# A fused decoder layer on one core: the self-attention's step rewritten with its mask added by VectorE, and the openings of three phases

## The chip, the cores and the metric

The kernel runs on one core of a Trainium2 chip. The metric is the time of one execution on the device in microseconds (us). TensorE (PE) multiplies matrices, VectorE (DVE), ScalarE (ACT) and GpSimd (POOL) work on tiles of 128 partitions, and SyncE (SP) issues most transfers between the chip's memory (HBM) and the core. Each engine runs its own queue of instructions in order; engines wait for each other through semaphores.

## The reference

One decoder layer, all in float32, for x of 4 x 512 tokens x 512 features:

```
x = x + self_attention(layernorm(x))
x = x + cross_attention(layernorm(x), ctx)
x = x + feed_forward(layernorm(x))

self_attention(h):                      # 16 heads of 128, one key and one value head
    q = rmsnorm(rope(h @ wq_comp @ wq_up)) * q_norm_w      # 16 heads
    k = rmsnorm(rope(h @ wk)) * k_norm_w;  v = h @ wv
    scores = q k^T / sqrt(128);  scores = where(0 <= i - j < 128, scores, -1e30)
    probs = softmax([scores, sink_logit])[..., :t]
    return (group_of_4_heads(probs @ v) @ out_w1[group]) @ out_w2
cross_attention(h, ctx):                # 16 query heads of 32, 4 key heads, 1024 keys
    softmax(q k^T / sqrt(32) + slope_h * (j - i), masked) @ v @ Wo
feed_forward(h):                        # 512 -> 2048 -> 512, 8-bit activations, ternary weights
    z = silu(bitlinear(h, w_gate)) * bitlinear(h, w_up)
    return bitlinear(fwht(z), w_down)   # fwht: Walsh-Hadamard transform over 2048
```

## The kernel before

The program has three phases, one after the other, each with a block of code per engine. Matrices that need float32 accuracy are kept as two rounded halves (`_hi`, made by ScalarE with a Copy, and `_lo`, the difference, made by VectorE), and a product is three matmuls, hi x hi, lo x hi and hi x lo (the helper `three`, L640 to L642).

**Self-attention** (`phase_self_attention`, L114) works on 16 tiles of 128 tokens. The window of 128 keys means that a tile sees its own 128 keys and the 128 before (256 keys in 12 of the tiles, 128 in the first tile of each batch of 512 tokens). A tile has 4 steps, one for each group of 4 heads, so there are 64 steps c = 0 to 63. Every engine's block runs the same loop `for c in CS` with c from -9 to 66 (L249), and in one pass of it does parts of several steps: the scores of step c, the query transposes of c+1, the probability transposes of c-1, the head outputs `ps_a` and the output product `ps_out` of steps before, the query projection `ps_up` of c+3, and on some steps the projections of a later tile. The order within a pass is the order of the code, and it sets the order on each queue.

The mask of a step is put down by TensorE: before the scores, two matmuls of the identity with the mask's window (`ident_r`, `window_r`, L690) write -1e30 or 0 into `ps_s`, and the score matmuls add to that. VectorE then takes the maximum of the four heads in one instruction (L538), forms the negated maximum times the norm factor (four small instructions, L542), ScalarE makes the exponentials (L442, one for each head), VectorE the reciprocal of the sum, GpSimd multiplies (L634) and TensorE transposes the result (L710).

In the opening (c = -8 to -1) TensorE also multiplies out_w1 by out_w2, so that the output product of a head is one matrix of 128 x 512: two heads in each pass (`merged_heads`, L257), 4 matmuls a head, in float32 (L674). The weights of a group of 4 heads are 2 MB, loaded in 2 transfers (`load_merge`).

**Cross-attention** (`phase_cross_attention`, L784) runs over 64 heads (4 batches x 16), each in 4 units of 128 queries; the scores of a unit are 2 matmuls of 512 keys. Scores are computed twice, once for the maximum (L1435, read by VectorE L1286) and once with the maximum folded in (L1418, read by ScalarE). Queries and keys are made by projections, split, stored to HBM in part and read back by SP into the stacked operands `Q` and `K` (`spread_queries`, `spread_keys`). In the opening the first head's queries are written into `Q` by ScalarE and VectorE; the others come by DMA. The rows of the next batch are loaded by `load_x1` (L924) and measured by VectorE (`statistics`, L1157).

**Feed-forward** (`phase_feed_forward`, L1513) runs over 16 tiles of 128 tokens, 4 quarters each. The last stages of the Walsh-Hadamard transform, sums and differences between quarters (`between_quarters`, L1783, into `fC` and `fA`) and between halves (`between_halves`, L1798, into `fB`), are made by GpSimd for every tile, and TensorE transposes `fB` (L1830).

The order in all three phases is written out by hand in these loops; there is no scheduler.

## Time and profile before

| | us |
|---|---|
| three runs | 1744.24, 1746.03, 1747.74 |
| median | 1746.03 |
| profiled execution | 1742.52 |
| its span | 1740.7 |
| PE busy | 1632.4 (94%) |
| DVE busy | 1202.6 (69%) |
| ACT busy | 1238.6 (71%) |
| POOL busy | 1184.2 (68%) |

The span is the time from the first to the last instruction that the profiler recorded; the profiled execution's own time is 1.8 us more. The self-attention takes the span's first 665 us or so, the cross-attention goes on to about 1400, and the feed-forward fills the rest. Busy shares are averages over these stages. The rows below come from four views: the busy time of each engine in stretches, instructions grouped by line, the waits of an engine, and the timeline of single stretches. In a row of the timeline the first number is the start, the second the duration of the whole entry (which may stand for several instructions, x2), and in square brackets stands how long the engine was idle before and what released it.

### The profile page before, as it was taken

What the parts mean: (1) busy time and instruction counts of PE and PEld (TensorE: products, weight loads), DVE (VectorE), ACT (ScalarE), POOL (GpSimd) and SP (SyncE); (2) the same over time, 40 slices, a digit from 0 to 9 for tenths busy, and PEclk for the clock granted to TensorE, in tenths of its full rate; (3) what the DMA queues carried; (4) which work ended last, traced back from release to release, by engine and by line L of the source; (5) the groups of instructions that cost most, each with busy time, mean ns of one, the idle gap of its engine ahead of it and who ended that gap; (6) DMA issues with size and microseconds to landing.
All of it is one profiled execution on the core that took longest, in us unless ns stands there. A gap on an engine that the chain in (4) does not pass through costs nothing. (4 is left out here: it accounts for less than half of the span.)

```text
span 1740.7 us, 24610 instructions
## 1 busy us (share of the span) xinstructions
PE 1632.4 (94%) x7920; PEld 1147.5 (66%) x7920; DVE 1202.6 (69%) x2284; ACT 1238.6 (71%) x2022; POOL 1184.2 (68%) x1085
## 2 busy tenths in 40 slices
PE   6999989999999997799999999999999977999996
PEld 3488878888888875566656665666556534666664
DVE  2378778677766665668787778777787735777764
ACT  2366577888666653589788778888897845787875
POOL 0377877777887762457666666666776739888892
PEclk9999999999999998899999999999999999999999
DMA  6214234333300102411141113101200320001000
GB/s 231 97 61 87 98 104 123 103 94 115 110 13 7 37 7 51 132 42 34 28 122 46 34 34 115 28 28 40 60 24 25 140 109 1 26 26 36 25 20 25
DMA packets 57215, 110.32 MB, mean 63 GB/s; under 512 B 9180, under 2 KB 13660, under 8 KB 56704
## 3 DMA queue, kind: packets, MB, share of 16 engines
q1 hardware_dynamic: 55536, 107.84, 20.1%
q8 instruction: 65, 1.06, 0.3%
q10 hardware_dynamic: 1552, 0.91, 0.2%
q14 instruction: 62, 0.51, 0.1%
HBM read 71.10 MB, written 18.88 MB: 52 GB/s over the span
## 5 line engine op out<-in xcount | busy, mean ns | idle before, releaser
L1351 POOL TENSOR_TENSOR x_p_lo<-x_p,x_p_hi 128x1024 fp32r<-128x1024 f32 x192 | 455.3, 2385 | 232.8 <-ACT x_p_hi L1148 232.4
L1286 DVE TENSOR_REDUCE x_maxes<-x_ps_a 128x1 f32<-128x1024 f32 x252 | 306.9, 1218 | 150.8 <-PE x_ps_a L1435 145.8
L1121 ACT ACTIVATE x_p<-x_ps_b,x_any_valid 128x1024 f32<-128x1024 f32 x256 | 285.1, 1114 | 128.8 <-PE x_ps_b L1418 113.7
L1418 PE MATMUL x_ps_b<-x_Q,x_K 100*128 100x512 f32 x512 | 228.1, 527 | 7.0 <-ACT x_p L1121 4.4
L1148 ACT ACTIVATE x_p_hi<-x_p 128x1024 fp32r<-128x1024 f32 x192 | 203.2, 1058 | 4.8
L1435 PE MATMUL x_ps_a<-x_K,x_Q 99*128 99x512 f32 x504 | 165.9, 410 | 11.2 <-DVE x_maxes L1286 9.0
L1464 PE MATMUL x_ps_o<-x_p_hi,x_V 128*96 128x512 f32 x384 | 156.7, 408 | 1.2 <-POOL x_p_lo L1351 1.2
L1418 PEld LDWEIGHTS x_ps_b<-x_Q,x_K 100*128 100x128 f32 x512 | 89.9, 191 | 99.8 <-issue 74.4
L1465 PE MATMUL x_ps_o<-x_p_lo,x_V 128*96 128x512 f32 x384 | 151.1, 393 | 0.0
L442 ACT ACTIVATE a_work<-a_ps_s,a_neg_max,a_q_r 128x256 f32<-128x256 f32 (+1 forms) x256 | 134.1, 540 | 4.6 <-DVE a_neg_max L542 4.6
L634 POOL TENSOR_TENSOR a_work<-a_work,a_inv_den 128x1024 f32<-128x1024 f32 (+1 forms) x64 | 110.0, 1719 | 18.6 <-DVE a_inv_den L582 18.6
L1435 PEld LDWEIGHTS x_ps_a<-x_K,x_Q 99*128 99x128 f32 x504 | 90.5, 191 | 48.0 <-DVE x_maxes L1286 26.9
L1469 PE MATMUL x_ps_o<-x_p,x_V 128*96 128x512 f32 x256 | 120.4, 591 | 0.0
L623 POOL TENSOR_TENSOR a_q_r<-a_q_ss,a_half_neg 128x4 f32<-128x4 f32 x64 | 65.2, 1018 | 75.5 <-DVE a_q_ss L560 73.8
L640 PE MATMUL a_ps_out<-a_w_hi,a_aT_hi 128*128 128x512 f32 x256 | 108.5, 424 | 1.4 <-DVE a_aT_lo L503 1.4
L642 PE MATMUL a_ps_out<-a_w_hi,a_aT_lo 128*128 128x512 f32 x256 | 102.9, 402 | 0.0
L641 PE MATMUL a_ps_out<-a_w_lo,a_aT_hi 128*128 128x512 f32 x256 | 102.5, 400 | 0.0
L427 ACT ACTIVATE a_qT_hi<-a_ps_front 128x512 fp32r<-128x512 f32 x64 | 38.3, 598 | 64.3 <-PE a_ps_front L701 64.3
L1296 DVE CAST x_Q<-x_ps_x 4x128 fp32r<-4x128 f32 x256 | 74.1, 289 | 9.3 <-PE x_ps_x L1447 1.3
L1464 PEld LDWEIGHTS x_ps_o<-x_p_hi,x_V 128*96 128x96 f32 x384 | 62.2, 162 | 26.5 <-POOL x_p_lo L1351 2.0
L609 POOL TENSOR_TENSOR a_work<-a_q 128x512 f32<-128x512 f32 x64 | 66.5, 1040 | 18.9 <-ACT a_q L465 18.9
L503 DVE TENSOR_TENSOR a_aT_lo<-a_ps_a,a_aT_hi 128x512 fp32r<-128x512 f32 x64 | 44.2, 691 | 49.5 <-ACT a_aT_hi L386 49.1
(254 smaller groups left out, 4353.3 us busy)
## 6 DMA issues: line engine op xcount, KB each, us to landing
shared<-in_L_attn_out_w SPq DMA_DIRECT2D x8, 1024.0 KB, 7.3
shared<-in_L_ffn_w_gate SPq DMA_DIRECT2D x16, 512.0 KB, 4.3
shared<-in_L_ffn_w_up SPq DMA_DIRECT2D x16, 512.0 KB, 4.1
shared<-in_L_ffn_w_down SPq DMA_DIRECT2D x16, 512.0 KB, 4.0
shared<-in_ctx SPq DMA_DIRECT2D x8, 1024.0 KB, 7.5
x_scratch<-rows SPq DMA_DIRECT2D x31, 256.0 KB, 2.0
x_Q<-x_q_hi SPq DMA_DIRECT2D x112, 64.0 KB, 2.0
ffn_quant<-shared SPq DMA_DIRECT2D x24, 256.0 KB, 4.6
```

Of the source, the lines that this page charges most:

```text
L442: act.activation(p[:, c % 2, j, 0:w], ps_s[:, j, 0:w], ACT.Exp, scale=q_r[:, c % 4, j:j + 1], bias=neg_max[:, c % 2, j:j + 1], accum_out=r ...
L634: pool.tensor_tensor(out=p[:, c % 2, :, 0:w], in0=p[:, c % 2, :, 0:w], in1=inv_den[:, c % 2, :].unsqueeze(2).to_broadcast([P, G1, w]), op= ...
L640: pe.matmul(out_ap, hi, rhs_hi, start=start, stop=False)
L1121: act.activation(p[:, r, :, :], ps_b[:, :, :], ACT.Exp, scale=any_valid[:, b % 2:b % 2 + 1]).then_inc(exp_ready, 1)
L1148: act.activation(p_hi[:, r], p[:, r], ACT.Copy).then_inc(hi_ready, 1)
L1286: dve.tensor_reduce(out=maxes[:, c % 2, 32 * r + 3:32 * r + 4], in_=scores_bank(n)[:, :, :], axis=mybir.AxisListType.XY, op=ALU.max).then_ ...
L1351: pool.tensor_tensor(out=p_lo[:, r], in0=p[:, r], in1=p_hi[:, r].bitcast(F32), op=ALU.subtract).then_inc(lo_ready, 1)
L1418: last = pe.matmul(ps_b[:, j, :], K[0:ROWS + 4, g, kb * P:(kb + 1) * P], Q[0:ROWS + 4, hh, :], start=True, stop=True)
L1435: last = pe.matmul(scores_bank(n)[:, j, :], Q[0:ROWS + 3, h2, r * P:(r + 1) * P], K[0:ROWS + 3, g2, j * 512:(j + 1) * 512], start=True, st ...
L1464: pe.matmul(bank[0:ROWS, :], vs, p_hi[:, rw, j], start=(rw == 0 and j == 0), stop=False)
L1465: last = pe.matmul(bank[0:ROWS, :], vs, p_lo[:, rw, j], start=False, stop=False)
L1469: last = pe.matmul(bank[0:ROWS, :], V32[:, bw % 2, j, gw, :], p[:, 3, j], start=False, stop=(j == 1))
```

## The change

It has five parts.

1. **Mask.** The two mask matmuls of each step and their operands go. The score matmuls start `ps_s` themselves. VectorE negates the window once, and in each step runs one `tensor_tensor_reduce` for each head, which adds the window to the scores in PSUM, writes them back there and takes their maximum.
2. **Order of a step.** On TensorE the head outputs `ps_a` of step c-2 come behind the scores of step c (they stood at the end of the pass before, as step c-1), and the output product of c-2 goes to the pass's end. The matching splits move on ScalarE and VectorE, the query's norm factor is negated one pass later, and GpSimd's power (`a_q_r`) comes behind its multiply.
3. **Opening of the self-attention.** The merge of the first group's 4 heads is all done at c = -8, chunk by chunk, each of 4 chunks (256 KB of out_w1 and 256 KB of out_w2) with a semaphore of its own, and without waiting for the constants; then two heads in each of c = -7 to -2, none at c = -1. Loads are issued in another order, and four splits are made later.
4. **Opening of the cross-attention.** Two heads' queries are written on the chip instead of one; the second query projection is cut into four pieces that stand between the scores of c = -2; SP loads the next batch's rows ahead of the last keys and Wo; the next batch's statistics start one head later.
5. **Feed-forward.** For tiles 0 and 15 the second `between_quarters` and both `between_halves` run on VectorE.

```diff
 # part 1, VectorE
-                    dve.tensor_reduce(out=s_max[:, c % 2, :], in_=ps_s[:, :, 0:w], axis=AXX, op=ALU.max).then_inc(s_max_ready, 1)
+                    for j in range(G1):
+                        dve.tensor_tensor_reduce(out=ps_s[:, j, 0:w], in0=ps_s[:, j, 0:w], in1=window[:, 2 * P - w:], scale=1.0,
+                                                 scalar=-3.0e38, op0=ALU.add, op1=ALU.max,
+                                                 accum_out=s_max[:, c % 2, j:j + 1]).then_inc(s_max_ready, 1)
 # parts 1 and 2, TensorE
-                    for j in range(0, G1, 2):
-                        pe.matmul(ps_s[:, j:j + 2, 0:w], ident_r[:, :], window_r[:, 2 * P - w:].unsqueeze(1).to_broadcast([P, 2, w]),
-                                  start=True, stop=False)
                     for j in range(G1):
                         last = three(ps_s[:, j, 0:w], qT_hi[:, c % 2, j, :], qT_lo[:, c % 2, j, :], kT_hi[:, keys], kT_lo[:, keys],
-                                     False, j % 2 == 1)
+                                     True, True)
...
 # part 2, VectorE
+                if 0 <= c - 2 < STEPS:
+                    k = c - 2
+                    dve.wait_ge(aT_hi_ready, k + 1)
+                    dve.tensor_tensor(out=aT_lo[:, k % 2, :], in0=ps_a[:, :], in1=aT_hi[:, k % 2, :].bitcast(F32), op=ALU.subtract)\
+                        .then_inc(aT_lo_ready, 1)
                 if 0 <= c + 1 < STEPS:
                     k = c + 1
+                    dve.wait_ge(q_r_ready, k + 1)
+                    dve.tensor_scalar(neg_r[:, k % 4, :], q_r[:, k % 4, :], -1.0, None, ALU.mult).then_inc(neg_r_ready, 1)
 # part 3, SyncE and TensorE
-            load_merge(0)
+            for k in range(DC):
+                sp.dma_start(w1_raw[:, 0, k, :], w1t[0, k * P:(k + 1) * P, :]).then_inc(w12_chunk_in[k], 16)
+                sp.dma_start(w2_raw[:, 0, k, :], w2[k * P:(k + 1) * P, :]).then_inc(w12_chunk_in[k], 16)
...
-            pe.wait_ge(const_in, 96)
-            pe.wait_ge(round_ready, 3)
             for c in CS:
-                for m in merged_heads(c):
+                if c == -8:
+                    for k in range(DC):
+                        pe.wait_ge(w12_chunk_in[k], 32)
+                        for m in merged_heads(c):
+                            last = pe.matmul(merge_bank(m), w1_raw[:, 0, k, m * P:(m + 1) * P], w2_raw[:, 0, k, :],
+                                             start=(k == 0), stop=(k == DC - 1))
...
+                    pe.wait_ge(const_in, 96)
+                    pe.wait_ge(round_ready, 1)
 # part 4, ScalarE, TensorE
+            act.wait_ge(first_q_made, 1)
+            for j in range(2):
+                act.activation(Q[0:DH, j, :], ps_j[j * DH:(j + 1) * DH, :], ACT.Copy, scale=QSCALE).then_inc(first_heads_hi_ready, 1)
...
                     if n == 4:
+                        pe.wait_ge(first_heads_dup_ready, 2)
+                        pe.wait_ge(first_heads_lo_ready, 2)
+                    if n == 8:
                         pe.wait_ge(q_spread[0], queries_spread(0, 0))
...
+                if c == -2:
+                    last = pe.matmul(ps_x[:, :], wq_sb[:, r, P:2 * P], hT[:, r, :], start=(r == 0), stop=(r == DC - 1))
 # part 5, VectorE (and the same condition negated on GpSimd)
+        VECTOR_TILES = (0, TILES - 1)
+                if i == 0 and quarter(c, 4) and n - 1 in VECTOR_TILES:
+                    between_quarters(dve, n - 1, 2)
+                if i == 1 and quarter(c, 5) and n - 1 in VECTOR_TILES:
+                    between_halves(dve, n - 1, 0)
+                    between_halves(dve, n - 1, 1)
```

TensorE's queue around the scores of a step in the self-attention's middle, before. The names are the product and its operands, so `a_ps_s` are scores, `a_ps_front` the query transposes, `a_ps_pT` those of the probabilities:

```order
L690 MATMUL a_ps_s<-a_window_r,a_ident_r 128x512 x2
L640 MATMUL a_ps_s<-a_kT_hi,a_qT_hi 128x256
L641 MATMUL a_ps_s<-a_kT_lo,a_qT_hi 128x256
L642 MATMUL a_ps_s<-a_kT_hi,a_qT_lo 128x256
...
L701 MATMUL a_ps_front<-ident,a_q 128x128 x4
L710 MATMUL a_ps_pT<-ident,a_work 128x128 x8
```

The same place after:

```order
L646 MATMUL a_ps_s<-a_kT_hi,a_qT_hi 128x256
L647 MATMUL a_ps_s<-a_kT_lo,a_qT_hi 128x256
L648 MATMUL a_ps_s<-a_kT_hi,a_qT_lo 128x256
...
L646 MATMUL a_ps_a<-a_pT_hi,a_v_hi 128x512
L647 MATMUL a_ps_a<-a_pT_lo,a_v_hi 128x512
L648 MATMUL a_ps_a<-a_pT_hi,a_v_lo 128x512
...
L722 MATMUL a_ps_front<-ident,a_q 128x128 x4
L731 MATMUL a_ps_pT<-ident,a_work 128x128 x8
```

The two mask matmuls are gone, and the six matmuls of `ps_a` (two blocks of keys, three each; one block is shown, and one head of the scores) now stand between the scores and the query transposes.

VectorE's queue in one step, before:

```order
L538 TENSOR_REDUCE a_s_max<-a_ps_s 128x4
L542 TENSOR_SCALAR a_neg_max<-a_s_max,a_neg_r,a_neg_sinks 128x1 x4
L547 TENSOR_TENSOR a_qT_lo<-a_ps_front,a_qT_hi 128x512
L553 TENSOR_TENSOR a_pT_lo<-a_ps_pT,a_pT_hi 128x1024
L558 TENSOR_REDUCE a_q_ss<-a_work 128x4
L560 TENSOR_SCALAR a_q_ss<-a_q_ss 128x4
L579 TENSOR_SCALAR a_neg_r<-a_q_r 128x4
L582 RECIPROCAL a_inv_den<-a_den 128x4
```

And after; the first two rows, an operation over one head's scores and the reading of its accumulator, stand four times in the queue:

```order
L537 ISA a_ps_s,a_s_max<-a_ps_s,a_window 128x256
L537 ISA a_s_max 128x1
...
L543 TENSOR_SCALAR a_neg_max<-a_s_max,a_neg_r,a_neg_sinks 128x1 x4
L548 TENSOR_TENSOR a_aT_lo<-a_ps_a,a_aT_hi 128x512
L553 TENSOR_SCALAR a_neg_r<-a_q_r 128x4
L555 TENSOR_TENSOR a_qT_lo<-a_ps_front,a_qT_hi 128x512
L560 TENSOR_REDUCE a_q_ss<-a_work 128x4
L562 TENSOR_SCALAR a_q_ss<-a_q_ss 128x4
L582 RECIPROCAL a_inv_den<-a_den 128x4
L587 TENSOR_TENSOR a_pT_lo<-a_ps_pT,a_pT_hi 128x1024
```

One instruction has become eight, the split of `ps_a` came down from ahead of them, and the split of the probabilities went behind the reciprocal.

## Rows read from the trace of the kernel before

**Rows 1.** Busy time by stretch; columns: stretch, length, engines (instructions), PE clock, DMA share, GB/s.

```profile
0.00:81.00 81.00, 64.66 (x176) 32.24 (x176) 23.02 (x51) 22.55 (x47) 13.85 (x30) 1.00 0.44 153
81.00:240.00 159.00, 149.16 (x863) 129.55 (x864) 126.68 (x284) 100.09 (x277) 124.94 (x192) 0.98 0.30 88
240.00:440.00 200.00, 186.70 (x1066) 162.01 (x1066) 148.18 (x351) 160.58 (x373) 152.98 (x233) 0.98 0.38 112
440.00:645.00 205.00, 198.50 (x1148) 171.36 (x1148) 137.61 (x321) 125.49 (x345) 158.15 (x235) 1.00 0.11 36
665.00:720.00 55.00, 39.96 (x149) 27.36 (x150) 35.40 (x55) 20.18 (x24) 16.08 (x9) 0.81 0.37 101
720.00:1380.00 660.00, 654.86 (x2495) 410.03 (x2494) 503.76 (x739) 549.59 (x598) 448.41 (x198) 1.00 0.19 56
```

**Rows 2.** Instructions by line, 80 to 660 us; busy total, mean ns, idle before.

```profile
L538 DVE TENSOR_REDUCE a_s_max<-a_ps_s 128x4 f32<-128x1024 f32 (+1 forms) x64 | 69.4, 1085 | 8.3 <-PE a_ps_s L642 8.2
...
L690 PE MATMUL a_ps_s<-a_window_r,a_ident_r 128*128 128x512 f32 (+1 forms) x128 | 36.9, 370 | 1.8 <-ACT a_work L442 0.9 <-DVE a_qT_lo L547 0.9
```

**Rows 3.** Waits of TensorE, 100 to 640 us; total us, times, longest.

```profile
PE a_ps_front L701 <- DVE a_kT_lo L523: 12.1, 13, 2.0
...
PE a_ps_front L701 <- DVE a_hT_lo L508: 3.8, 13, 0.6
...
PE a_ps_front L701 <- DVE a_v_lo L513: 2.9, 1, 2.9
```

**Rows 4.** Timeline of one step of the self-attention and the start of the next.

```profile
442.62 0.62 PE L690 MATMUL a_ps_s<-a_window_r,a_ident_r 128*128 128x512 f32 x2
443.08 0.28 PE L640 MATMUL a_ps_s<-a_kT_hi,a_qT_hi 128*128 128x256 f32 x1
...
444.71 1.23 DVE L538 TENSOR_REDUCE a_s_max<-a_ps_s 128x4 f32<-128x1024 f32 x1 [0.16 <-PE a_ps_s L642]
445.97 0.82 DVE L542 TENSOR_SCALAR a_neg_max<-a_s_max,a_neg_r,a_neg_sinks 128x1 f32<-128x1 f32 x4
...
447.63 0.56 ACT L442 ACTIVATE a_work<-a_ps_s,a_neg_max,a_q_r 128x256 f32<-128x256 f32 x1
...
453.62 0.28 DVE L520 TENSOR_TENSOR a_qcT_lo<-a_ps_front,a_qcT_hi 128x128 fp32r<-128x128 f32 x1
453.82 0.28 DVE L523 TENSOR_TENSOR a_kT_lo<-a_ps_front,a_kT_hi 128x128 fp32r<-128x128 f32 x1
```

**Rows 5.** Busy time by stretch, the first 10 us.

```profile
0.00:5.00 5.00, 0.00 (x0) 0.00 (x0) 0.09 (x2) 0.71 (x1) 0.20 (x4) 1.00 0.52 160
5.00:10.00 5.00, 0.00 (x0) 0.00 (x0) 0.00 (x0) 0.57 (x1) 0.00 (x0) 1.00 1.04 369
```

**Rows 6.** Timeline of the self-attention's opening.

```profile
15.46 8.65 PE L674 MATMUL a_ps_s<-shared 128*128 128x512 f32 x16 [15.46 <-ACT a_window_r L374]
...
26.00 1.90 DVE L478 TENSOR_TENSOR a_w_lo<-a_work,a_w_hi 128x512 fp32r<-128x512 f32 x3 [0.53 <-ACT a_w_hi L378]
...
80.91 0.50 PE L690 MATMUL a_ps_s<-a_window_r,a_ident_r 128*128 128x256 f32 x2 [0.87 <-DVE a_qT_lo L547]
...
82.78 1.00 DVE L579 TENSOR_SCALAR a_neg_r<-a_q_r 128x4 f32<-128x4 f32 x1 [1.13 <-POOL a_q_r L623]
```

**Rows 7.** Timeline of the cross-attention's opening.

```profile
679.56 3.60 PE L1398 MATMUL x_ps_x<-x_hT,shared 128*128 128x512 f32 x8
...
689.56 1.22 PE L1435 MATMUL x_ps_a<-x_K,x_Q 99*128 99x512 f32 x2 [1.99 <-DMA x_Q<-x_p_lo]
...
711.88 0.69 DVE L1157 BATCH_NORM_STATS2 x_stats<-shared 128x6 f32<-128x512 f32 x1 [9.37 <-DMA shared<-x_scratch]
...
713.96 1.22 PE L1435 MATMUL x_ps_a<-x_K,x_Q 99*128 99x512 f32 x2 [5.26 <-DVE x_maxes L1286]
```

**Rows 8.** Timeline of the feed-forward's first tile.

```profile
1440.55 1.27 POOL L1788 TENSOR_TENSOR f_fC<-f_f 128x512 f32<-128x512 f32 x1
...
1445.70 4.66 POOL L1801 TENSOR_TENSOR f_fB<-f_fA 128x1024 f32<-128x1024 f32 x2
1448.09 0.66 PE L1830 MATMUL f_ps_t<-ident,f_fB 128*128 128x128 f32 x4 [4.53 <-POOL f_fB L1801]
```

More of the change, by code:

```diff
@@ L214, in phase_self_attention @@
         w12_in = [sem(f"w12_in{j}") for j in range(2)]
+        w12_chunk_in = [sem(f"w12_chunk_in{k}") for k in range(DC)]
         x_in = [sem(f"x_in{j}") for j in range(XR1)]
@@ L762, in _ @@
                     last.then_inc(qckT_made, 1)
[L763 to L772 removed]
+                if 0 <= c - 2 < STEPS:
+                    k = c - 2
+                    t, g = divmod(k, 4)
+                    pe.wait_ge(aT_lo_ready, k + 1)
+                    if g == 0 and t:
+                        pe.wait_ge(x1_ready, t)
+                    for j in range(G1):
+                        hh, cols = G1 * g + j, slice(j * P, (j + 1) * P)
+                        last = three(ps_out[:, :], aT_hi[:, k % 2, cols], aT_lo[:, k % 2, cols], w12_hi[:, hh, :], w12_lo[:, hh, :],
+                                     hh == 0, hh == H1 - 1)
+                    if g == 3:
+                        last.then_inc(out_made, 1)
 HX, HPG, DH = 16, 4, 32
@@ L967, in spread_queries @@
                 hi, lo = q_stage(g, b)
-                for j in range(1 if b == g == 0 else 0, HPG):
+                for j in range(2 if b == g == 0 else 0, HPG):
                     rows = slice(j * DH, (j + 1) * DH)
@@ L1353, in _ @@
                     normalise((c - 8) // HPG)
-                if 0 <= c < HEADS and b + 1 < B and (hh, r) == (1, 0):
+                if 0 <= c < HEADS and b + 1 < B and (hh, r) == (1 if b else 2, 0):
                     deviations(b + 1)
```

250 lines of the change are left out of this document (120 added, 130 removed).

## The prediction

> **What bounds the kernel now.** I read the busy time by stretch first. TensorE is busy for 149 of 159 us, 187 of 200 and 198.5 of 205 in the self-attention, and for 655 of 660 in the cross-attention's long middle [rows 1]. The change does not touch that middle, so what it can give lies in the self-attention, in the two openings (65 of 81 us, 40 of 55) and at the feed-forward's ends. The grouping by line then gives the price of the mask on TensorE and of the maximum on VectorE [rows 2], TensorE's waits say what it stands for inside the self-attention [rows 3], and the timelines show one step and the three places in the openings [rows 4, 6, 7, 8]. A step lasts (646 - 81) / 64 = 8.83 us. VectorE, which gets the new work, is the next engine: 80% busy from 81 to 240, 74% to 440, 67% to 645 [rows 1], which is 7.1, 6.55 and 5.9 us of a step.
>
> **Self-attention, what goes from TensorE.** With two blocks of keys, the mask's two matmuls start at 442.62 and the scores at 443.08: 0.46 us of the queue [rows 4]. 48 steps of this form give 22.1 us; the 16 steps with one block write half as much, about 0.3 each, 4.8 us. That is 27 us; the row of the line says 36.9 over 128 matmuls [rows 2], but those durations overlap the next matmul, so I go by the starts. TensorE is the busiest engine and in order, so this is taken from the path unless something else becomes late.
>
> The new place of ps_a fills a hole. TensorE waits for the splits of a tile's projections before its query transposes: 12.1 + 3.8 + 2.9 = 18.8 us in 27 waits [rows 3], none over 2.0 us but one. The six matmuls of ps_a (c-2), 6 x 0.23 = 1.4 us at the spacing of the mask's 512-wide ones (0.46 for two [rows 4]), stand in front of these transposes now and need only what is older. 18.8 us is the most they can hide, and 1.4 x 27 covers most of it. Together -45.8 is the lower end.
>
> **What VectorE takes on.** One maximum of 1.23 us [rows 4] becomes four passes over 128 x 256 with a second operand, and four accumulator reads. No such instruction is in the trace. The nearest rows: two 128 x 128 subtractions from PSUM start 0.20 apart, at 453.62 and 453.82 [rows 4]; three 128 x 512 ones take 1.90, 0.63 each [rows 6]. A straight line between them puts 256 columns at 0.35, and a 128 x 1 instruction of the kind behind neg_max costs 0.82 / 4 = 0.2 [rows 4], as an upper value for the accumulator read; 0.07 is what a read could cost if it ran beside the next pass. So 0.42 to 0.55 a head, 1.7 to 2.2 a step. I take 2.0, against 1.23: +0.8 us on VectorE a step. The other bound is a pass at half the rate because it reads PSUM, reads SBUF and writes PSUM: 0.63 + 0.2 = 0.83 a head, 3.3 a step. There is no gain below 1.23, as the same columns go through with more instructions.
>
> The rows show that a second short instruction starts before the first one's 0.28 us are over: starts 0.20 apart [rows 4]. The Trainium skill (VectorE: DVE Perf Modes, "Rules for kernel authors") advises to minimize the number of chained VectorE operations, because each pays for its pipeline's flush; that speaks against making eight of one. By it a head would cost its full duration, about 0.42, and a full 0.2 for the read, near 0.6, 2.5 us a step, between my value and the upper bound. The Trainium skill (Vector Engine (DVE) Microarchitecture Reference, "7. Points that are easy to get wrong") says that this family of operations halves its throughput with two SBUF sources that are not bf16; here one source is in PSUM, so it should be spared, and if the rule holds for this pair too the result is the second rival below. No row here shows either.
>
> With +0.8, VectorE needs 7.9 us of a step early and 6.7 late, where TensorE alone would take about 8.83 - 45.8 / 64 = 8.1. At 94% and above VectorE's order delays what TensorE waits for. I set this friction at 0.35 us for the first 18 steps (6.3) and 0.17 for the other 46 (7.8), 14 us, an estimate from the present gaps: today at 80% the loss of TensorE is 10 of 159 us [rows 1], 0.55 a step. The cycle that could bind instead is scores of step c, maximum, neg_max, exponentials, scores of c+1: 1.45 + 2.0 + 0.82 + four exponentials of 0.56 [rows 4] + some 0.35 of hand-over = 6.9 us, below 8.4; up to 3.4 us of masked maximum it does not decide. Moving the split of the probabilities behind the reciprocal and the negated factor one pass later costs no instruction: TensorE needs pT_lo only for ps_a, which is now a whole pass later, and the wait for GpSimd's power, 1.13 us in the opening [rows 6], goes. GpSimd loses nothing.
>
> Self-attention: -27 - 19 + 14 = **-32** (from -45 to +3, the upper end with the pass at 0.83).
>
> **Opening of the self-attention.** TensorE starts at 15.46, released by the constants' last copy [rows 6]. After, it needs x's first transfer, whose 0.26 MB go ahead, and the first chunk, 0.52 MB; the constants' 0.58 MB travel beside them, so 0.78 to 1.38 MB must land. 160 GB/s in the first 5 us are 0.80 MB, and then 369 GB/s [rows 5]: from 5.0 to 6.6 us. I take 6.2, -9.3 us at the start. A chunk comes every 0.52 MB / 369 GB/s = 1.42 us and TensorE needs 8.65 / 16 x 4 = 2.2 us for its 4 matmuls [rows 6], so nothing waits behind. Then the last pass has no merges, which stood beside the chain from projection to the first scores (they wait 0.87 us for qT_lo at 80.91 already [rows 6]); about 2 us come back there. **-7** (from -9.3 to -3).
>
> **Opening of the cross-attention.** From 665 to 720 TensorE is idle for 15.0 of 55 us, and the clock is at 0.81, between its levels of 1.2 and 2.4 GHz [rows 1]. Three things go: the second projection, 3.6 us in the row at 679.56, leaves the way to the first scores and fills the gaps of the pass c = -2 (worth 1.5, as the keys' splits come after it anyway); the wait of 1.99 us for the first DMA of `x_Q` at 689.56; and the wait of 5.26 us at 713.96, which follows VectorE's 9.37 us for the next batch's rows [rows 7]. SP now issues these loads before the last keys, and the statistics come one head later, some 5 us. I count 5.3 + 2.0 + 1.5 = 8.8, and with fewer gaps 1.2 of the clock's loss: **-10**. At -4 the wait at 713.96 only moves to the keys (0,2), which now stand behind four loads of 256 KB; at -16 most of the idle time goes.
>
> **Feed-forward.** For tile 0 GpSimd needs from 1440.55 to 1445.70 for the quarters and 4.66 for both halves; TensorE starts 4.53 us late at 1448.09 [rows 8]. VectorE makes the four quarter operations at 0.63 each [rows 6], 2.5 us, with a product of 0.7 among them, then a half (twice the columns) at 1.2: the first half is there at about 1445.1, -3. Tile 15 does the same by the same code near the very end, where I count -1. VectorE's other work there is that product and small rows. **-4** (-8 to -1).
>
> **Sum.** 1742.5 - 32 - 7 - 10 - 4 = 1689.5 by the profiled execution. The median of the runs is 3.5 us above that execution, so I predict 1689.5 + 3.5 = 1693 us.
>
> **Rivals.**
> - *VectorE's pass is slow.* At 0.83 a head a step needs 9.2, 8.7 and 8.0 us of VectorE, with hand-overs 9.4, 8.9 and 8.5: 18 x 9.4 + 22.6 x 8.9 + 23.4 x 8.5 = 569 us, against 565 now: the self-attention gives about nothing. 1742.5 - 21 + 3.5 = 1725. For it: VectorE is at 80% early, and PSUM is read and written. Against it: a subtraction with one source in PSUM and one in SBUF starts its successor after 0.20 us for 128 columns [rows 4], and one with both in SBUF takes 0.63 for 512 [rows 6], on one line.
> - *The openings give little.* The first chunk lands late or the chain before the first scores is what counts (-3), and the keys (0,2) take the place of the rows' wait (-3), -2 in the feed-forward: 1742.5 - 40 + 3.5 = 1706.
> - *Slower.* The masked pass costs over 0.93 us a head, 3.7 a step: then VectorE needs 9.2 us a step on average (5.3 for the rest, 3.7, and 0.2), 0.33 over today's 8.83, and 64 x 0.33 = 21 us eat the other three gains. This is the turning point. At 1.1 a head it is 64 x 0.9 = +57 -21 = +36: 1782. For it speaks only that no row shows a PSUM-to-PSUM pass with an accumulator.
>
> **Chances.** The forecast 0.62 (its own range 1679 to 1711); the slow pass 0.20; small openings 0.12; slower 0.06. For 8 in 10 the range goes from 1675 to 1724: it leaves out the slower case, half of the slow pass and the gain of all lower ends together. 0.2% of this kernel, 3.5 us, is what a measurement can tell from no change. Slower by more 0.05, within 0.02, faster 0.93.
>
> **What would show it.** In the profile after: the pass of 128 x 256 at about 0.35 us from start to start, with a read of 0.07 to 0.2 behind it; VectorE at 90% or more of the first 160 us of steps; a step at 8.3 to 8.4 us; TensorE's waits for kT_lo below 6 us in all; the first matmul at 6 to 7 us; the first scores at 72 to 75; no wait over 3 us between 700 and 720 of the old time; the first transpose of fB 3 us earlier relative to its tile. It is wrong if TensorE waits for `a_neg_max` or `a_qT_lo` on most steps, if the exponentials start over 4.5 us after the scores' end, or if the cross-attention's middle takes another time than 655 to 660 us, which nothing here foresees.

## The result, and the profile after

The changed kernel takes 1719.76 us (median of 4 runs, 1718.59 to 1720.79) against 1745.13 of the kernel before beside it: the ratio is 0.9852, 95% interval 0.9835 to 0.9869. Its profiled execution has a span of 1716.7 us, 24.0 less than before. The forecast was 1693 us: the direction was right, the gain was half of what was forecast (25 us of 53).

The span can be cut at the same instructions in both traces: the first scores (74.63 us after, 80.91 before [rows 6]), the cross-attention's first matmul, the start of its last row of four matmuls in the timeline (1419.06 before, 1397.96 after), and the end.

| | before | after | change | forecast |
|---|---|---|---|---|
| start to first scores | 80.9 | 74.6 | -6.3 | -7 |
| self-attention's steps | 584.2 | 581.1 | -3.2 | -32 |
| cross-attention | 753.9 | 742.3 | -11.6 | -10 |
| feed-forward | 321.6 | 318.7 | -2.9 | -4 |

Three terms came out nearly as sized, one of them in part by luck (the cross-attention, see below). One did not: the self-attention. The busy time by stretch, with the columns of [rows 1], shows why it isn't that the mask's work stayed:

```profile
81.00:240.00 159.00, 143.45 (x823) 122.25 (x822) 136.47 (x411) 100.23 (x279) 124.29 (x195) 0.97 0.30 81
240.00:440.00 200.00, 179.16 (x1029) 151.34 (x1028) 156.27 (x497) 157.05 (x368) 152.75 (x234) 0.99 0.35 107
440.00:640.00 200.00, 187.84 (x1095) 159.35 (x1094) 147.61 (x485) 121.82 (x346) 152.49 (x231) 1.00 0.11 36
```

TensorE was busy for 149.16 and 186.70 us in the first two stretches and is now for 143.45 and 179.16: it has less to do and is idle for longer. The granted clock is no rival here: it is 0.97 to 1.00 in these stretches, and 0.98 to 1.00 in the same ones before. VectorE rose from 80 to 86% in the first stretch, from 74 to 78% in the second. TensorE's waits from 100 to 640 us name what it is idle for:

```profile
PE a_ps_front L770 <- DVE a_qT_lo L555: 15.2, 14, 3.3
PE a_ps_front L751 <- DVE a_qT_lo L555: 13.6, 13, 1.7
PE a_ps_front L646 <- DVE a_qT_lo L555: 10.6, 13, 1.4
PE a_ps_out L646 <- DVE a_aT_lo L548: 4.6, 8, 0.9
PE a_ps_front L722 <- DVE a_v_lo L511: 1.2, 2, 0.6
```

The 18.8 us of [rows 3] are 1.2 now, as forecast. But 39.4 us in 40 waits for `a_qT_lo` stand in their place, and there were none of them in that stretch before. 29 of the 40 last 0.5 to 1.3 us; the longest, 3.3 us, is in step 20. L751, L646 and L770 are the three pieces of a tile that share the bank `ps_front` with the query transposes: the transposes of h, the projections, the transposes of the compressed queries and keys. One timeline of a step shows the mechanism (compare with [rows 4]):

```profile
438.85 0.28 PE L648 MATMUL a_ps_s<-a_kT_hi,a_qT_lo 128*128 128x256 f32 x1
...
439.17 0.43 DVE L537 CUSTOM_DVE_ANT_0 a_ps_s<-a_ps_s,a_window 128x256 f32<-128x256 f32 x1
...
439.52 0.14 DVE L537 DVE_READ_ACCUMULATOR2_ANT a_s_max<- 128x1 f32 x1
439.52 0.47 DVE L537 CUSTOM_DVE_ANT_0 a_ps_s<-a_ps_s,a_window 128x256 f32<-128x256 f32 x1
...
439.90 0.47 DVE L537 CUSTOM_DVE_ANT_0 a_ps_s<-a_ps_s,a_window 128x256 f32<-128x256 f32 x1
...
440.84 0.82 DVE L543 TENSOR_SCALAR a_neg_max<-a_s_max,a_neg_r,a_neg_sinks 128x1 f32<-128x1 f32 x4
...
441.58 0.68 DVE L548 TENSOR_TENSOR a_aT_lo<-a_ps_a,a_aT_hi 128x512 fp32r<-128x512 f32 x1
...
442.24 0.69 DVE L555 TENSOR_TENSOR a_qT_lo<-a_ps_front,a_qT_hi 128x512 fp32r<-128x512 f32 x1
...
443.08 0.41 PE L770 MATMUL a_ps_front<-ident,shared 128*128 128x128 f32 x2 [0.55 <-DVE a_qT_lo L555]
443.24 0.48 PE L646 MATMUL a_ps_out<-a_w_hi,a_aT_hi 128*128 128x512 f32 x1
```

The masked maximum goes from 439.17 to 440.84, 1.67 us, with starts 0.38 apart for each head and its read beside the next pass: cheaper than the 2.0 of the forecast. From the scores' end at 439.1 VectorE needs 3.8 us until `a_qT_lo` is complete at 442.93. TensorE has only ps_a, two groups of transposes and ps_up to do meanwhile (3.4 us) and then comes to the tile's piece, where it waits. The 2.9 us of output product, which the piece doesn't need, stand behind the piece since the change.

### The profile page after: what moved, and what is told of

The parts are those of the page before. It is cut to its first block and busy times, and to the rows that moved or that the text cites. A ratio compares the mean times of both kernels' runs of the same rounds, so it can differ in the third digit from the quotient of the medians.

```text
span 1716.7 us, 24811 instructions
## 1 busy us (share of the span) xinstructions
PE 1603.6 (93%) x7792; PEld 1114.6 (65%) x7792; DVE 1233.5 (72%) x2746; ACT 1230.5 (72%) x2022; POOL 1159.8 (68%) x1073
## 5 line engine op out<-in xcount | busy, mean ns | idle before, releaser
L425 ACT ACTIVATE a_aT_hi<-a_ps_a 128x512 fp32r<-128x512 f32 x64 | 38.3, 598 | 153.9 <-PE a_ps_a L648 153.8
L437 ACT ACTIVATE a_work<-a_ps_s,a_neg_max,a_q_r 128x256 f32<-128x256 f32 (+1 forms) x256 | 134.2, 535 | 11.7 <-DVE a_neg_max L543 9.7
L537 DVE CUSTOM_DVE_ANT_0 a_ps_s<-a_ps_s,a_window 128x256 f32<-128x256 f32 (+1 forms) x256 | 92.4, 423 | 52.0 <-PE a_ps_s L648 51.8
L636 POOL TENSOR_TENSOR a_work<-a_work,a_inv_den 128x1024 f32<-128x1024 f32 (+1 forms) x64 | 107.6, 1681 | 32.8 <-DVE a_inv_den L582 32.8
L1458 PEld LDWEIGHTS x_ps_a<-x_K,x_Q 99*128 99x128 f32 x504 | 91.1, 189 | 35.9 <-DVE x_maxes L1304 12.1
L646 PE MATMUL a_ps_out<-a_w_hi,a_aT_hi 128*128 128x512 f32 x256 | 106.0, 414 | 6.5 <-DVE a_aT_lo L548 6.5
L587 DVE TENSOR_TENSOR a_pT_lo<-a_ps_pT,a_pT_hi 128x1024 fp32r<-128x1024 f32 (+1 forms) x64 | 69.4, 1084 | 16.0 <-ACT a_pT_hi L447 15.3
```

Of the source, the lines that this page charges most:

```text
L437: act.activation(p[:, c % 2, j, 0:w], ps_s[:, j, 0:w], ACT.Exp, scale=q_r[:, c % 4, j:j + 1], bias=neg_max[:, c % 2, j:j + 1], accum_out=r ...
L636: pool.tensor_tensor(out=p[:, c % 2, :, 0:w], in0=p[:, c % 2, :, 0:w], in1=inv_den[:, c % 2, :].unsqueeze(2).to_broadcast([P, G1, w]), op= ...
L646: pe.matmul(out_ap, hi, rhs_hi, start=start, stop=False)
L1458: last = pe.matmul(scores_bank(n)[:, j, :], Q[0:ROWS + 3, h2, r * P:(r + 1) * P], K[0:ROWS + 3, g2, j * 512:(j + 1) * 512], start=True, st ...
```

## The experiments

All were run beside the kernel before. The kernels' rows of waits are of the stretch 100 to 640 us. Each time is compared with the kernel before by a ratio of medians, with its 95% interval; the medians of the kernel before in the rounds are 1741.95 to 1745.13 us. For the comparison by steps, this is the time from the start of one step's scores to another's in the profiled executions, with TensorE's busy and idle time over steps 0 to 61 (the mask's matmuls count to the scores):

| us | steps 0-15 | 16-39 | 40-61 | TensorE busy, 0-61 | idle |
|---|---|---|---|---|---|
| before | 141.0 | 220.7 | 192.2 | 524.9 | 29.0 |
| changed kernel | 142.0 | 220.9 | 188.0 | 500.4 | 50.5 |
| mask_on_pe | 142.9 | 216.5 | 191.8 | 523.6 | 27.6 |
| mask_only | 143.6 | 223.6 | 195.5 | 505.3 | 57.5 |
| out_first | 135.1 | 214.7 | 180.2 | 502.6 | 27.4 |
| qt_first | 140.6 | 220.4 | 190.1 | 511.0 | 40.0 |
| out_first_mask_pe | 135.4 | 210.3 | 185.1 | 518.6 | 12.2 |
| mask_pe_plus_pass | 138.1 | 214.8 | 188.6 | 522.8 | 18.7 |
| hybrid | 132.8 | 210.4 | 180.2 | 510.9 | 12.5 |
| at_before_neg | 134.2 | 219.6 | 186.2 | 507.2 | 32.8 |

**out_first.** The output product ahead of the tile's pieces:

```diff
-                t = tile_of(c, 7)        # and tile_of(c, 6), tile_of(c, 4): the tile's pieces
-                ...
                 if 0 <= c - 2 < STEPS:
                     k = c - 2
                     t, g = divmod(k, 4)
                     pe.wait_ge(aT_lo_ready, k + 1)
                     ...
+                t = tile_of(c, 7)        # the pieces, unchanged, now behind
+                ...
```

> The changed kernel with one move on TensorE: the output product of c-2 stands ahead of the tile's pieces (transposes of h, projections, transposes of q/k compressed) and no longer behind them. Theory (the gain was eaten by a wait on an order): after the change these 48 pieces wait 15.2 + 13.6 + 11.9 = 40.7 us for qT_lo, which VectorE now makes behind the masked maximum and aT_lo; 2.9 us of output product in front of them cover that wait (0.85 us each). Expected: waits for qT_lo under 8 us, the self-attention 20 to 32 us shorter, 1690 to 1700 us. Rival (VectorE's load of the masked maximum is the limit): the wait only moves to the output product or to the next scores, and the time stays within 4 us of 1720.

Measured: 1697.72 us, ratio 0.9736 (0.9719 to 0.9754), some 20 us below the changed kernel. No wait for `a_qT_lo` is left in TensorE's list; its largest row is

```profile
PE a_ps_out L646 <- DVE a_aT_lo L548: 22.8, 35, 2.0
```

The cause is shown: one move on TensorE's queue gives back most of what was missing, with the same work on every engine. By the table the steps 0 to 61 are 21.0 us shorter and TensorE is idle for 23.1 us less. The rival, that VectorE's load alone sets the pace, does not hold for these 20 us, but about half of the wait moved to `a_aT_lo`.

**qt_first.** The two blocks exchanged on VectorE:

```diff
-                (aT_lo of c-2)
                 (neg_r and qT_lo of c+1)
+                (aT_lo of c-2)
```

> The changed kernel with one move on VectorE: neg_r and qT_lo of c+1 ahead of aT_lo of c-2. Theory (wait on an order): qT_lo comes 0.7 us earlier, of 0.85 us waited on average in 48 pieces, about -25 us; but aT_lo comes 0.9 later and in the 16 steps without a piece the output product starts right behind ps_up, so up to 0.8 us comes back in each, +13: 1705 to 1712 us. Rival (load): no change, 1716 to 1723.

Measured: 1718.66 us, ratio 0.9860 (0.9841 to 0.9878), no change from the changed kernel, in the range of the rival.

```profile
PE a_ps_out L646 <- DVE a_aT_lo L555: 16.0, 21, 1.5
PE a_ps_front L770 <- DVE a_qT_lo L550: 6.3, 6, 2.2
PE a_ps_front L646 <- DVE a_qT_lo L550: 5.7, 7, 1.0
PE a_ps_front L751 <- DVE a_qT_lo L550: 4.7, 8, 1.0
```

A miss of the expectation. The waits for `a_qT_lo` fell from 39.4 to 16.7, those for `a_aT_lo` rose from 4.6 to 16.0, as the mechanism says; the sum is 11 us lower, and yet the time is the same. TensorE's busy time from 81 to 640 us is 9.8 us more (520.25 against 510.45) for the same instructions. A step of this trace shows where most of it goes, beside the step of the changed kernel above:

```profile
436.36 0.28 PE L648 MATMUL a_ps_s<-a_kT_hi,a_qT_lo 128*128 128x256 f32 x1
...
440.04 0.67 DVE L555 TENSOR_TENSOR a_aT_lo<-a_ps_a,a_aT_hi 128x512 fp32r<-128x512 f32 x1
...
440.26 0.41 PE L770 MATMUL a_ps_front<-ident,shared 128*128 128x128 f32 x2 [0.22 <-DVE a_qT_lo L550]
440.76 0.50 PE L646 MATMUL a_ps_out<-a_w_hi,a_aT_hi 128*128 128x512 f32 x1
```

The tile's piece waits 0.22 us and not 0.55, but the output product behind it now starts 0.50 us after it and not 0.16: it needs `a_aT_lo`, which is complete at 440.71. This second wait stands inside the recorded durations of the transposes, so the list of waits has no entry for it and the busy time takes it in. From the scores' end (436.64 and 439.13) to the start of the output product it is 4.12 us here and 4.11 in the changed kernel. The output product itself needs `a_aT_lo`, and the piece ahead of it on the queue needs `a_qT_lo`, so it comes behind both, and the order of the two on VectorE does not change when the second is done: the rival's result, but for a reason of order. The granted clock has a part in the longer busy time too: by the trace's records of it, it is at the lower of its levels for 20.5 us of steps 0 to 61 here and for 13.7 in the changed kernel, which is worth at most 3.4 us (an estimate, half of the difference).

**mask_on_pe and mask_only.** The mask's part of the diff undone in the changed kernel, and done alone in the kernel before:

```diff
 # mask_on_pe, TensorE and VectorE
+                    for j in range(0, G1, 2):
+                        pe.matmul(ps_s[:, j:j + 2, 0:w], ident_r[:, :], window_r[:, 2 * P - w:]..., start=True, stop=False)
-                    for j in range(G1):
-                        dve.tensor_tensor_reduce(out=ps_s[:, j, 0:w], in0=ps_s[:, j, 0:w], in1=window[:, 2 * P - w:], ...)
+                    dve.tensor_reduce(out=s_max[:, c % 2, :], in_=ps_s[:, :, 0:w], axis=AXX, op=ALU.max).then_inc(s_max_ready, 1)
 # mask_only: the same lines the other way, in the kernel before
```

> The changed kernel with the mask back on TensorE (two matmuls of identity and window a step, one maximum over 4 heads on VectorE); order, openings and feed-forward as changed. Theory (wait on an order): only the 16 steps without a tile's piece lose the 0.46 us, +7; in the 48 others the maximum is 0.44 us shorter and TensorE 0.46 later, so most of the wait for qT_lo is gone and the step stays as it is, 0 to +5: 1725 to 1732 us. Rival (the mask's 27 us were really gained and lost again through the new order): +20 to +27, 1740 to 1747.

> The kernel before with the mask alone moved to VectorE; order, openings and feed-forward as before. Theory (wait on an order): in the old order the output product stands in front of the tile's pieces and covers VectorE, so the 27 us of TensorE are mostly gained: -15 to -25, 1720 to 1730 us. Rival (VectorE's load is the limit): within 6 us of 1745, or slower.

Measured: mask_on_pe 1718.54 us, ratio 0.9855 (0.9836 to 0.9873), the changed kernel's time; mask_only 1753.16 us, ratio 1.0059 (1.0040 to 1.0078), slower than before by 7 to 14 us. So the mask's move, from which the forecast took 27 us, is worth nothing in the new order, and is a loss in the old one. mask_on_pe lies 7 us below its expectation, mask_only 23 above (its rival, no gain or slower, holds): I had still given the move too much. The waits of mask_on_pe say where the 27 us went in the new order:

```profile
PE a_ps_front L773 <- DVE a_qT_lo L555: 9.5, 14, 2.2
PE a_ps_front L754 <- DVE a_qT_lo L555: 8.5, 13, 1.2
PE a_ps_front L646 <- DVE a_qT_lo L555: 4.9, 13, 1.1
```

With the mask on TensorE 22.9 us of waits for `a_qT_lo` are left; with it on VectorE they are 39.4. So 22.9 us belong to the order of the queues alone and 16.5 to the masked passes. By the table the move spares TensorE 23.2 us of work in steps 0 to 61 and adds 22.9 us of idle time. In most of the 48 steps with a tile's piece VectorE is the later of the two already without the masked passes, so what they add is waited for in full.

The waits of mask_only show who pays in the old order; they were 12.1 and 3.8 [rows 3] for `a_kT_lo` and `a_hT_lo`, and 3.7 for `a_work`:

```profile
PE a_ps_front L698 <- DVE a_kT_lo L520: 19.8, 14, 3.0
PE a_ps_pT L707 <- POOL a_work L634: 13.7, 17, 1.1
...
PE a_ps_front L698 <- DVE a_hT_lo L505: 9.2, 13, 0.8
```

**out_first_mask_pe.** Both edits: the good order, the mask on TensorE.

```diff
 # out_first's move on TensorE, and mask_on_pe's lines
```

> out_first (output product ahead of the tile's pieces) with the mask back on TensorE and the single maximum on VectorE; against out_first it prices the mask's move in an order without the wait for qT_lo. Theory (the move is worth TensorE's 27 us less what VectorE's 0.44 us more a step costs): in out_first 22.8 us are waited for aT_lo in 35 steps; with a maximum 0.44 us shorter some 15 of them go, so +12, 1706 to 1714 us. Rival 1 (full gain in this order): +20 to +27, 1718 to 1725. Rival 2 (the move is worth nothing in any order, as mask_on_pe against the changed kernel): 1696 to 1700.

Measured: 1700.53 us, ratio 0.9744 (0.9729 to 0.9759). Against out_first's 0.9736 that is the same; the theory's 1706 to 1714 us is missed. The wait for `a_aT_lo` went down as expected, by 16 us:

```profile
PE a_ps_out L646 <- DVE a_aT_lo L548: 6.7, 12, 1.4
```

The second rival holds for the whole (1700.5 for 1696 to 1700): TensorE has 16.1 us less to do in steps 0 to 61 with the mask on VectorE, and is idle for 15.2 us more. But the table by steps shows that the zero is a sum: with the mask on VectorE, steps 40 to 61 are 4.9 us shorter and steps 16 to 39 are 4.4 us longer. VectorE also works through the feed-forward's weights in steps 17 to 40, with a pass that stands just ahead of the masked maximum (L502, 0.4 us and more), but another pass over them, of 1.2 us (L565), stands in steps 1 to 23, and over steps 0 to 15 the two kernels take the same time. So that these weights are the reason is not shown. A single step without a tile's piece takes 7.68 us with the mask on VectorE and 8.08 with it on TensorE, late in the phase (step 43, for one): that 0.40 is the mask's price, where TensorE sets the pace.

**mask_pe_plus_pass.** One more VectorE instruction a step, nothing taken from TensorE; the output is the same:

```diff
                     dve.tensor_reduce(out=s_max[:, c % 2, :], in_=ps_s[:, :, 0:w], axis=AXX, op=ALU.max).then_inc(s_max_ready, 1)
+                    dve.wait_ge(s_max_ready, 2 * c + 1)
+                    dve.tensor_reduce(out=s_max[:, c % 2, 0:1], in_=ps_s[:, 0, 0:w], axis=AXX, op=ALU.max).then_inc(s_max_ready, 1)
...
```

> out_first_mask_pe (good order, mask on TensorE) with one more VectorE instruction in each step: the maximum of the first head's 128 x 256 scores taken a second time into the same place, some 0.38 us ahead of neg_max; no other work changes. It loads VectorE as the masked pass does, without taking anything from TensorE. Theory (VectorE's 0.44 us a step eats the 27 us that TensorE saves): +15 to +25 us against out_first_mask_pe, 1715 to 1725. Rival (TensorE's mask matmuls were never worth 27 us, because something else paces the steps): +0 to +7, 1700 to 1708 us.

Measured: 1709.84 us, ratio 0.9813 (0.9800 to 0.9826), which is 12 us over out_first_mask_pe by the ratios (9 by the medians). The instruction delays the next one by 0.46 us:

```profile
447.14 0.42 DVE L541 TENSOR_REDUCE a_s_max<-a_ps_s 128x1 f32<-128x256 f32 x1
447.60 0.82 DVE L545 TENSOR_SCALAR a_neg_max<-a_s_max,a_neg_r,a_neg_sinks 128x1 f32<-128x1 f32 x4
```

It lies between the two expectations, below the theory's. At most 64 x 0.46 = 29 us of VectorE cost 12 us of time, although VectorE was busy for 79% only (444 of 559 us, 87% in the first stretch). So 0.46 us more a step on VectorE costs about 12 us even when TensorE keeps its work. The rest of the 27 is accounted for by both together, which no run takes apart: where VectorE paces a step, what TensorE is spared gives nothing.

**hybrid.** out_first with the mask placed by step:

```diff
+        def mask_on_pe(c):
+            return c < 4 or 16 <= c < 40 or c % 4 == 2
...
+                    if mask_on_pe(c):
+                        dve.tensor_reduce(out=s_max[:, c % 2, :], in_=ps_s[:, :, 0:w], ...)
+                    else:
+                        (the four masked passes, with window_r as the second operand)
...
-                    for j in range(0, G1, 2):
+                    for j in range(0, G1, 2) if mask_on_pe(c) else []:
```

> out_first with the mask on TensorE in steps 0 to 3, 16 to 39 and every step with c mod 4 = 2 (where VectorE carries the feed-forward's weights or TensorE carries a tile's projections), and on VectorE in the others. Theory (the move pays 0.4 us a step where VectorE has room and costs where it has not): by the steps of out_first and out_first_mask_pe the range 16 to 39 is 4.4 us shorter with the mask on TensorE, 0 to 15 and 40 to 61 are 5 us shorter with it on VectorE: 4 to 7 us below out_first, 1691 to 1694 us, below both. Rival (the differences between those two are not of single steps but of the balance over several): no better than the better of the two, 1697 to 1700 us.

Measured: 1692.72 us, ratio 0.9714 (0.9701 to 0.9728). By the table it has the shorter time of either kernel in each range, to 0.1 us, and 2.3 us less in steps 0 to 15. It beats the kernel before by 50 us and the changed kernel by some 24, and the intervals of the latter's ratio and its own are far apart. Against out_first the medians differ by 5.0 us and the intervals overlap by 0.0009; the difference is in the range expected, but the time alone does not settle it.

**at_before_neg.** out_first, with `aT_lo` moved between the masked maximum and neg_max on VectorE:

```diff
                     (the four masked passes)
+                if 0 <= c - 2 < STEPS: (aT_lo of c-2)
                     dve.wait_ge(s_max_ready, 4 * c + 4)
                     (neg_max)
-                if 0 <= c - 2 < STEPS: (aT_lo of c-2)
```

> out_first with aT_lo of c-2 on VectorE between the masked maximum and neg_max. Theory (what is left is the order on VectorE): aT_lo comes 0.8 us earlier less 0.2 for its wait on aT_hi; of the 22.8 us waited for it 12 to 16 go, while the exponentials start 0.9 us later, which the step's cycle (scores 1.45, maximum 1.6, aT_lo 0.9, neg_max 0.8, exponentials 2.3, hand-overs 0.4 = 7.5 of 7.7 to 8.7 us) just holds: 1683 to 1690 us. Rival (the cycle is full): TensorE waits for the exponentials before the scores or GpSimd's product before the transposes, 1697 to 1715 us.

Measured: 1712.55 us, ratio 0.9816 (0.9799 to 0.9833), 15 us slower than out_first. The theory fell, the rival's size holds, but the wait isn't one of the two it named:

```profile
PE a_ps_a L648 <- DVE a_pT_lo L589: 18.4, 30, 2.2
PE a_ps_out L648 <- DVE a_aT_lo L543: 5.7, 10, 1.6
```

The exponentials come later, so ScalarE's pT_hi, so VectorE's pT_lo, and TensorE waits for it before ps_a: ScalarE waits 67.6 us for `a_neg_max` in this stretch, 19.1 in out_first.

**late_rows.** In the changed kernel, the next batch's rows behind the keys and Wo again, and the statistics one head earlier:

```diff
-            (wait for x1_stored and first_norm_made; load_x1(1, 0..3))
             spread_keys(0, 2)
             spread_keys(0, 3)
             sp.dma_start(wo_sb...)
+            (wait for x1_stored and first_norm_made; load_x1(1, 0..3))
...
-                    first = 0 if b else 1
+                    first = 0
```

> The changed kernel with the next batch's rows loaded behind the last keys and Wo again, and their statistics one head earlier again, as before; the two heads on the chip and the cut projection stay. Theory (the 5.3 us that TensorE waited at 713.96 went by this pair): 5 to 7 us of the cross-attention's 11.6 come back, 1724 to 1727 us. Rival (the wait would have gone with the shorter opening anyway): 1719 to 1722.

**old_cross.** The changed kernel with the whole function of before:

```diff
-def phase_cross_attention(...)   # of the changed kernel
+def phase_cross_attention(...)   # of the kernel before
```

> The changed kernel with the whole cross-attention phase of before. By the two traces its phase went from 753.9 to 742.3 us, 11.6. Theory (the gain is the opening's own): 1729 to 1733 us. Rival (part of it comes from what the self-attention leaves behind, such as its last stores or TensorE's clock): 1722 to 1727.

Measured: late_rows 1728.52 us, ratio 0.9917 (0.9904 to 0.9931), above its 1724 to 1727; old_cross 1731.48 us, ratio 0.9923 (0.9908 to 0.9938), as expected. The whole part is worth some 12 us, as its trace says, and 9 to 11 of them (medians, ratios) go with where the rows are loaded and measured; the loads and the statistics were moved back together, so the two are not told apart. The timeline of late_rows, VectorE and TensorE:

```profile
703.36 0.69 DVE L1173 BATCH_NORM_STATS2 x_stats<-shared 128x6 f32<-128x512 f32 x1 [12.27 <-DMA shared<-x_scratch]
```

```profile
705.43 1.22 PE L1458 MATMUL x_ps_a<-x_K,x_Q 99*128 99x512 f32 x2 [9.18 <-DVE x_maxes L1304]
```

With the rows late, the wait is 9.18 us and not the 5.26 of [rows 7]: what the other edits of the part save ahead of it is waited for there again. In the changed kernel TensorE has no wait up to 735 us after

```profile
692.48 2.08 PE L1389 MATMUL x_ps_j<-shared 128*128 128x128 f32 x8 [2.02 <-DVE x_V L1216]
```

The phase has one edit more, which none of the five parts names and which neither run takes by itself. VectorE copies the slopes into the row maxima once for each of the 64 heads, and since the change does it with a maximum over one element:

```diff
-                dve.tensor_copy(at[:, :, 0:3], slope_cols[:, c % HX, 0:3].unsqueeze(1).broadcast_to([P, TPB, 3])).then_inc(slope_ready, 1)
+                dve.tensor_reduce(out=at[:, :, 0:3], in_=slope_cols[:, c % HX, 0:3].unsqueeze(1).broadcast_to([P, TPB, 3]).unsqueeze(3),
+                                  axis=AXX, op=ALU.max).then_inc(slope_ready, 1)
```

Its rows from 800 to 1400 us, before and after (busy total, mean ns):

```profile
L1223 DVE COPY x_maxes<-x_slope_cols 128x12 f32<-128x12 f32 x53 | 19.8, 373 | 0.0
```

```profile
L1239 DVE TENSOR_REDUCE x_maxes<-x_slope_cols 128x12 f32<-128x12 f32 x51 | 7.9, 155 | 0.0
```

The phase's traces can be cut at the first matmul of the second scores of head 5, 100 us in. From there to the phase's last matmul it is 655.4 to 655.5 us in the three kernels with the old function (before, mask_only, old_cross) and 651.6 to 651.8 in the eleven with the new one, late_rows among them. So 3.8 of the 11.6 us were gained in the middle of the phase. That the slopes' operation is the cause is not shown; it is the only edit there that recurs for every head. Up to head 5 it is 99.8 us before, 92.0 in the changed kernel, 100.7 in old_cross and 104.1 in late_rows: with the rows late, the opening's other edits make it no shorter.

**const_first.** The constants waited for ahead of the chunks:

```diff
+            pe.wait_ge(const_in, 96)
+            pe.wait_ge(round_ready, 1)
             for c in CS:
                 if c == -8:
...
-                    pe.wait_ge(const_in, 96)
-                    pe.wait_ge(round_ready, 1)
```

> The changed kernel with TensorE waiting for the constants again before the first merge; the chunks, the order of the loads and all else stay. In the changed kernel ScalarE has the constants at 12.9 us and TensorE starts at 7.28. Theory (TensorE is the path of the opening, so its start counts one for one): start at 13.3, first scores 5 to 6 us later, 1724 to 1727 us. Rival (the chain of a tile's projection, its norms and qT_lo sets the first scores): +0 to +2, 1719 to 1722 us.

Measured: 1725.38 us, ratio 0.9906 (0.9890 to 0.9923). The changed kernel's first matmul and its first scores, and then const_first's:

```profile
7.28 3.78 PE L676 MATMUL a_ps_s<-shared 128*128 128x512 f32 x4 [7.28 <-DMA shared<-in_L_attn_out_w]
...
74.63 0.33 PE L646 MATMUL a_ps_s<-a_kT_hi,a_qT_hi 128*128 128x128 f32 x1 [0.72 <-DVE a_qT_lo L555]
```

```profile
12.92 3.75 PE L678 MATMUL a_ps_s<-shared 128*128 128x512 f32 x4 [12.92 <-ACT ident_bf L376]
...
80.05 0.33 PE L646 MATMUL a_ps_s<-a_kT_hi,a_qT_hi 128*128 128x128 f32 x1 [0.71 <-DVE a_qT_lo L555]
```

A start 5.64 us later moves the first scores by 5.42: TensorE is the path of this opening, the theory holds, and the time is in the range expected.

**no_vector_tiles.** `VECTOR_TILES = ()` in the changed kernel.

```diff
-        VECTOR_TILES = (0, TILES - 1)
+        VECTOR_TILES = ()
```

> The changed kernel with all butterflies on GpSimd again (no tile's on VectorE). By the two traces the feed-forward gained 2.9 us. Theory: 1721.5 to 1724. Rival (the gain at the ends comes from the phase before, and VectorE is as slow here as GpSimd): 1719 to 1721.

Measured: 1720.19 us, ratio 0.9860 (0.9844 to 0.9877) against 0.9852 (0.9835 to 0.9869): inconclusive by the time (it lies in the rival's range, but a gain of 2.9 us would be hard to see in these runs). By the traces the wait of 4.53 us for fB is back, and the feed-forward takes 322.6 us against 318.7; the other phases differ between the two executions by as much, though their code is the same (the cross-attention by 2.5 us).

```profile
1422.61 1.12 PE L1867 MATMUL f_ps_t<-ident,f_fB 128*128 128x128 f32 x4 [4.53 <-POOL f_fB L1651]
```

## Why the prediction was off, step by step

**The opening** was right in mechanism and size: first matmul at 7.28 for 6.2, first scores 6.3 us earlier for 7. The 1.9 us lost on the way were forecast as 2 us, but all at the end; 0.9 of them are at the start, where the first four records of matmuls take 3.57 us and the next four 2.36, against 1.72 later; that is 2.5 us lost, and the kernel before loses 1.6 in its own first matmuls. The first records start 0.85 to 1.0 us apart and the later ones 0.43, half the rate, while the profile shows a granted clock of 1.00. The prediction's price of a chunk was too low: its four matmuls are eight records in the trace, 4.3 us at 8.65 / 16 each and not 2.2, which only makes it surer that TensorE does not wait for the next chunk.

**The cross-attention** was right in size (-11.6 for -10), in part by luck. The prediction said that the change does not touch the phase's middle and named another time there as a sign of being wrong; the middle is 3.8 us shorter, beside an edit that the description left out. The opening itself gave 7.8 (99.8 to 92.0 us). Its sum was made wrongly too: four savings were added, and late_rows shows that the whole of it hangs on the rows' place and that the others give nothing without it, since they stand ahead of a wait for a transfer that ends at its own time. What the early rows give without the other edits was not run. The clock's share was counted at 1.2 us; the granted clock rose from 0.81 to 0.88 in the phase's first 55 us, up to 3.9 us (an estimate, 0.07 x 55).

**The feed-forward** came out at -2.9 for -4 in the trace; the time can't tell.

**VectorE's price** was slightly too high: 1.67 us for four heads against 2.0, so the rival of the slow pass, 0.83 a head, is refuted, though the time lies near the 1725 it gave. It was near for another reason. The rival of a slower kernel is refuted with it; its sums were off besides, as 5.3 + 3.7 + 0.2 is 0.37 over 8.83 and not 0.33, and at 1.1 a head it is 1.07 and not 0.9. The Trainium skill's advice to minimize the count of chained VectorE operations (VectorE: DVE Perf Modes, "Rules for kernel authors"), as the prediction priced it, would have given 2.5: the trace has the next pass start 0.38 us after the one before, ahead of its 0.47's end, and the accumulator's read beside it. The halving for two SBUF sources (Vector Engine (DVE) Microarchitecture Reference, "7. Points that are easy to get wrong") did not appear with one source in PSUM; that section speaks of one instruction format, and whether this pass, which the trace names as a custom instruction, belongs to it no run here shows.

**The self-attention** is where it failed, in the term "friction". Two of its three numbers held: the mask's matmuls went, 0.40 us a step where TensorE sets the pace (the prediction had 0.46), and the waits for the projections' splits fell by 17.6 of 18.8. The third was an estimate of 14 us from VectorE's load; the waits measured are 39.4 for `a_qT_lo` and 4.6 for `a_aT_lo`, 44 us. It had to be read from the order, not from the load. The trace of the kernel before and the prediction's own price of the pass held most of it: masked maximum 1.67 to 2.0, neg_max 0.82, aT_lo 0.68, neg_r 0.07 to 0.3, qT_lo 0.69 are 4 us behind the scores, while TensorE has 1.4 + 0.44 + 0.8 + 0.7 = 3.4 us up to the tile's piece. In the steps in which TensorE needs these 3.4 us the waits are mostly 0.5 to 1.1 us; around a batch's first tile, with its 128 keys, it is at the piece after 2.3 to 3.0 us and waits for 0.6 to 2.2. The 40 waits, 1.0 us on average, are the 39 us. The prediction said that the output product went to the pass's end, and counted only what the new place of ps_a covers; it didn't ask what the output product had covered at its old place. That is the step that failed: the term "friction", put at 14 us from VectorE's load, stood for a wait on the order of two queues that took 44 us, and moving the output product ahead of the pieces (out_first) gives 20 to 22 us of it back. It did name "TensorE waits for `a_qT_lo` on most steps" as what would show it wrong, and that is what the profile shows: 40 such waits in the 60 or so steps from 100 to 640 us.

Even with this mended the 27 us of the mask were not there to be had: the term was right as work that TensorE is spared (23 to 24 us in steps 0 to 61) and wrong as a gain in time. Three pairs of kernels say so: its move is worth +10 us in the old order, 0 in the new, -1.4 (within the error) in out_first, and in single ranges of the last from -4.9 to +4.4. In the new order TensorE's idle time grew by as much as its work shrank, 23 us. What stays open is how the loss in steps 16 to 39 divides between VectorE's queue and the engines that it feeds.

Of the other signs named ahead, VectorE at 90% in the first 160 us and a step at 8.3 to 8.4 us did not come: it was at 86%, and a step takes 8.89 us (550.9 / 62).

## What to carry to other kernels

When a block is moved in an engine's queue, list what it covered at its old place as well as what it covers at the new one, and add up the other engine's chain to that point instruction by instruction: here VectorE's 3.8 us stood against TensorE's 3.4 or less in 48 steps, and that was 20 to 22 of the 29 us that were missing in this phase. Work moved from the busiest engine to the next one pays only in those steps where the first sets the pace; decide it by step and not for a whole phase. To exchange two operations on an engine gives nothing where the other engine's queue needs both before it can go on (qt_first): look for what needs the last of them. Savings ahead of a wait that ends at its own time (a transfer's) don't add: move that transfer first.

## What the runs showed of the hardware

A VectorE pass that reads PSUM and SBUF, writes PSUM and gives an accumulated maximum takes 0.38 us from start to start for 128 x 256 float32, and reading the accumulator (0.14 us) lies beside the next pass. With VectorE busy for 79% of the steps' time, 0.46 us more a step cost 12 us in 64 steps though TensorE was the busier engine (97%, 540.51 of 559 us). Writing 12 values on each of 128 partitions took VectorE 373 ns as a copy and 155 ns as a maximum over one element. TensorE's first matmul records of 128 x 512 float32 started 0.85 to 1.0 us apart for the first four in the kernel before and the first six in the changed one, then 0.43 us apart, with the granted clock shown as 1.00.
